# A four-layer graph network on one core: the first group's front begun before the other weights are prepared

## The chip, the cores and the metric

The kernel runs on one core of one Trainium2 chip. The metric is the device time of one execution in microseconds (us). TensorE is called PE here, ScalarE ACT, VectorE DVE, GpSimd POOL and SyncE SP; each has its own stream of instructions, and they meet only in semaphores.

## The reference, cut to what matters

There are 64 graphs of 128 nodes with 256 features, each with a 128x128 adjacency matrix and a node mask. Every graph goes through four layers, each followed by a layer norm over the features of input plus layer:

```
x = norm(x + attention(x, adj, mask, W_qkv, W_out, b_out))   # 8 heads of 64; 0.33*(softmax + adj + exp(-adj)) @ v
x = norm(x + hypergraph(x, adj, W1, b1, gamma, beta, W2, b2))
x = norm(x + diffusion(x, adj, Wv, bv, aw, ab, Wk[0..2], bk))
x = norm(x + relu([x, adj @ x / deg] @ W3.T))
```

All weights are shared by all graphs. They come as plain float32 and the kernel uses them in another form.

## The kernel before, in words

**Tiling.** Two graphs make a group (G = 2), 32 groups in all. The work on a group has a front (the attention layer and the adjacency statistics) and a back (the other three layers). In the steady state one pass of the loop runs the front of group i together with the back of group i-1, interleaved by hand. `group(i, j, n)` on every engine writes such a pass: front of i, back of j, and the first transposes and query/key products of n. The program is: set-up, `group(0, None, 1)` (a front alone), `group(1, 0, 2)`, a hardware loop over 29 more, and two passes at the end.

**Prepared weights.** Each weight matrix is kept as two float32r matrices, a high part (a copy by ACT, `set_hi` counts them) and a low part (weight minus high part, by DVE, `set_lo`; three of them by POOL, `set_pool_lo`). The list `splits` holds them in order: two pieces of W_qkv for queries and keys, two for values, W1, W3, W_out, W2, Wk, and two tiny ones for the gates. Some need more first. W1, W2 and W3 are transposed on PE with the identity (L424, L430, L436). W2 is centred with a row product (L455) that DVE adds (L1082), and the row product with beta (L459) makes `bw_bc`. W3 is centred on DVE (L1058 to L1066). Wk is centred with a column sum on PE (L465, L467), added by DVE (L1072, L1075). The gate vectors come from products on POOL (L1578, L1580), reductions and small sums on DVE (L1088 to L1099) and a column sum on PE (L473).

**The order of set-up.** Engines run their streams in the order in which they are written. PE's `set_up` does the three groups of transposes, waits until the first eight splits are done, transposes x and adj of group 0 (L486, L479), does query/key products 0 and 1 of group 0 (L497, L498, L501), and then the row products and column sums. Behind it each engine calls `set_up_done`, which waits for every split, every copy and every small result. Only then comes `group(0, None, 1)`: query/key products 2 and 3; the masks on ACT (L822, L826) and the gate (L814); scores S of graph 0 and 1 (L523, L531); values v (L408 to L412); the row maximum on DVE (L1197); exp on ACT (L853); normalisation `norm_` on DVE (L1210, eight instructions for a graph); transposes PT (L541) and their copy on ACT (L860); the product with v, PV (L551); its split (L865, L1123); W_out, W_ (L408 to L412); the sum y0 and norm (L1221, L1225, L1133, POOL L1595 to L1602, ACT L871); then AT_ (L516), adjT_ (L479) and ax_ (L571).

**Requests and memory.** SP issues the loads: W_qkv, W2, W1, W3, then adj, row weights, x and mask of group 0, then the gate vectors' inputs, W_out and Wk; ACT and POOL issue some small ones. All raw weights lie in the memory of the work tiles from `work_base` on, which the front of group 0 would write. `early_base` holds the few tiles (adjT, xT0, qk) that may be written during set-up.

Of the kernel before, what the change touches and what calls it, by code (L numbers as in the profile page):

```python
# [14 lines left out]
P = 128  # L15
HEADS = 8
# [10 lines left out]
def gnn_stack_kernel(nc, x, adj, nodemask, W_qkv, W_out, b_out, W1, b1, gamma, beta, W2, b2,  # L27
# [18 lines left out]
    with ctx:  # L46
# [49 lines left out]

        adjTb = at("adjTb", [P, G, P])
        gate = at("gate", [P, G, P])
        aT = pair("aT", [P, G, P])
# [4 lines left out]
        xT2 = pair("xT2", [P, DC, G, P])  # L104
        prob = at("prob", [P, 2, HEADS, P])
        probT = at("probT", [P, G, HEADS, P])
        oT = pair("oT", [P, G, IC, P])
        ys0 = at("ys0", [P, G, D])
        ysb = at("ysb", [P, G, D])
        x1t = at("x1t", [P, G, D])  # L110
        x2 = at("x2", [P, G, D])
        x3 = at("x3", [P, G, D])
        xout = at("xout", [P, G, D])
        resid = at("resid", [P, G, D])
        axT = pair("axT", [P, G, DC, P])
        hid = at("hid", [P, G, DHID])
        hT = pair("hT", [P, G, HC, P])
        hw = at("hw", [P, G, D])
        z01 = at("z01", [P, G, 2, D])
        e1 = at("e1", [P, G, P])  # L120
        e2 = at("e2", [P, G, P])
        al = at("al", [P, G, P])
        alT = pair("alT", [P, G, P])
        yv = at("yv", [P, G, D])
        yT = pair("yT", [P, G, D])
        za = at("za", [P, G, D])
        zb = pair("zb", [P, G, D])
# [16 lines left out]


        NORM0, NORMH, NORM1, NORM2, NORM3 = range(5)
        st = at("st", [P, 5, G, 6])
        mv = at("mv", [P, 5, G, 2])
        rs = at("rs", [P, 5, G, 2])

# [7 lines left out]
        wqkv_raw = at("wqkv_raw", [P, DC, HEADS, 3, DH])  # L158
        wout_raw = at("wout_raw", [P, IC, D])
# [26 lines left out]
        bA, bB, bD, bC, bE, bP, bQ, bR = range(8)  # L186
        bank_wk01, bank_wk2 = 6, 4
# [106 lines left out]
        SET_W2T, SET_W1, SET_W3, SET_CM, SET_BW, SET_WK, SET_MASK, SET_WJ = 1, 2, 3, 4, 5, 6, 7, 8  # L294
        FIRST_FROM_PSUM = len(splits)
        for c in range(DC):
            splits.append((PS[:, 2 + c, :], w1t[0][:, c], w1t[1][:, c], 0.5, (set_pe, SET_W1)))
        for c in range(DC):
            splits.append((PS[:, 4 + c, :].rearrange("p (t o) -> p t o", t=2), w3t[0][:, c], w3t[1][:, c], None,
                           (set_pe, SET_W3)))  # L300
        FIRST_DERIVED = len(splits)
        splits.append((wout_raw[:], wout[0][:], wout[1][:], MIX, (ld_wout, 16)))
        for k in range(HC):
            splits.append((w2c[:, k], w2t[0][:, k], w2t[1][:, k], None, (set_w2c, k + 1)))

        FIRST_ON_POOL = len(splits)
# [3 lines left out]
        POOL_SPLITS = range(FIRST_ON_POOL, len(splits))  # L310
# [36 lines left out]
        def _(sp):  # L347
            sp.dma_start(wqkv_raw[:].rearrange("p c h t d -> p c (h t d)"),
                         W_qkv.rearrange("(c p) n -> p c n", p=P)).then_inc(ld_wqkv, 16)
            sp.dma_start(w2_raw[:], W2.rearrange("(c p) n -> p c n", p=P)).then_inc(ld_w2, 16)  # L350
            sp.dma_start(w1_raw[:], W1.rearrange("(c p) n -> p c n", p=P)).then_inc(ld_w1, 16)
            sp.dma_start(w3_raw[:], W3.rearrange("(c p) n -> p c n", p=P)).then_inc(ld_w3, 16)

            def load_group(i):
                sp.dma_start(adj_in[:], ag[:, bass.ds(i * G, G), :]).then_inc(a_in, 16)
                sp.dma_start(wrow[:], adj[bass.ds(i * G, G), 0:1, :].rearrange("g a m -> (a g) m").partition_broadcast(P))\
                    .then_inc(w_in, 16)
                sp.dma_start(xin[:], xg[:, bass.ds(i * G, G), :]).then_inc(x_in, 16)
                sp.dma_start(mask_bc8[:], mask_rows[bass.ds(i, 1), :].rearrange("a n -> (a n)").partition_broadcast(P))\
                    .then_inc(m_in, 16)  # L360

            load_group(0)
# [4 lines left out]
            sp.dma_start(wout_raw[:], W_out.rearrange("(c p) n -> p c n", p=P)).then_inc(ld_wout, 16)  # L367
            for k in range(3):
                sp.dma_start(wk_raw[:, k], Wk[k].rearrange("(c p) n -> p c n", p=P)).then_inc(ld_wk, 16)
# [35 lines left out]
        def _(pe):  # L405
# [13 lines left out]
            def set_up():  # L419
                pe.wait_ge(ident_ok, 2)  # L420
                pe.wait_ge(ld_w2, 16)
                for k in range(HC):
                    for c in range(DC):
                        last = pe.transpose(PS[:, bQ + k // 2, (k % 2) * D + c * P:(k % 2) * D + (c + 1) * P],  # L424
                                            w2_raw[:, c, k * P:(k + 1) * P], ident[:])
                last.then_inc(set_pe, 1)
                pe.wait_ge(ld_w1, 16)
                for c in range(DC):
                    for k in range(HC):
                        last = pe.transpose(PS[:, 2 + c, k * P:(k + 1) * P], w1_raw[:, k, c * P:(c + 1) * P], ident[:])  # L430
                last.then_inc(set_pe, 1)
                pe.wait_ge(set_w3c, 4)
                for c in range(DC):
                    for t in range(2):
                        for o in range(DC):
                            last = pe.transpose(PS[:, 4 + c, t * D + o * P:t * D + (o + 1) * P],  # L436
                                                w3_raw[:, o, t * D + c * P:t * D + (c + 1) * P], ident[:])
                last.then_inc(set_pe, 1)


                pe.wait_ge(set_copy, 1)
                pe.wait_ge(set_hi, FIRST_DERIVED)
                pe.wait_ge(set_lo, FIRST_DERIVED)
                xT0_(0)
# [597 lines left out]
        def _(dve):  # L1042
# [3 lines left out]
            def set_up():  # L1046
# [55 lines left out]
                for n, (src, hi, lo, factor, (ready, value)) in enumerate(splits):  # L1102
                    if n == FIRST_FROM_PSUM:
                        rows()
                        centre_w3()
# [613 lines left out]
```

## Time and profile before

| what | value |
|---|---|
| median of 3 runs | 1316.94 us (1316.85 to 1317.2) |
| the profiled execution's own time | 1311.29 us |
| its span, first to last instruction | 1309.3 us |
| PE busy | 1251.3 us (96%) |
| DVE, ACT, POOL busy | 1070.5, 973.2, 479.4 us |
| mean granted TensorE clock | 0.987 |

The profile is of one execution. A timeline row gives start, length, engine, line, operation, output and inputs with their sizes, how many instructions are merged, and in brackets how long the engine had been idle and what released it. The granted clock is a share of full speed: 1.00 is 2.4 GHz, 0.50 is 1.2 GHz. Ends of matmuls are modelled, so rows of PE overlap a little; the spacing of starts is the better measure.

### The profile page before, as it was taken

The page shows a single profiled execution, that of the slowest core. Times are in us where ns is not written, and L with a number is a line of the kernel's source. Part 1 is how long each engine was busy: PE and PEld are TensorE (multiplying, and loading weights), DVE is VectorE, ACT ScalarE, POOL GpSimd, SP SyncE. Part 2 cuts the span into 40 slices and gives each one's busy share as a digit, 9 for nine tenths or more (in the row PEclk, how much of TensorE's full clock was granted, in tenths as well). Part 3 has the DMA queues.
Part 4 walks back from the last instruction along what each step waited for, and adds up shares of the span by engine and source line. Part 5 has one row for each costly group of instructions (what it writes and reads, how often), then busy time and mean ns, then how long its engine had stood idle before and what let it go on. Part 6 is the DMA issues. An engine that isn't in the chain of part 4 may idle for free.

```text
span 1309.3 us, 32907 instructions
## 1 busy us (share of the span) xinstructions
PE 1251.3 (96%) x9589; PEld 1112.7 (85%) x9589; DVE 1070.5 (82%) x3399; ACT 973.2 (74%) x2806; POOL 479.4 (37%) x1126
## 2 busy tenths in 40 slices
PE   3699999999999999999999999999999999999996
PEld 3588898888888888889898888988888888888874
DVE  3668898888889888888888888988888898888885
ACT  3467777787777778777878777777877777787773
POOL 2233333344433334343334433333444333343432
PEclk8799999999999999999999999999999999999998
DMA  6000000000000000000001100000001000000000
GB/s 202 10 18 27 26 9 17 25 25 25 25 17 17 17 25 25 25 25 8 23 19 25 25 25 25 8 19 23 25 25 25 20 13 17 25 25 25 17 9 9
DMA packets 44293, 32.52 MB, mean 25 GB/s; under 512 B 8176, under 2 KB 43120, under 8 KB 44272
## 3 DMA queue, kind: packets, MB, share of 16 engines
q1 hardware_dynamic: 42688, 31.47, 8.4%
q0 software_dynamic: 176, 0.52, 0.2%
q10 hardware_dynamic: 1408, 0.27, 0.1%
q8 instruction: 10, 0.16, 0.1%
q14 instruction: 11, 0.09, 0.0%
HBM read 23.87 MB, written 8.39 MB: 25 GB/s over the span
## 4 chain that ended last, share of the span: by engine, by line
PE 88%; issue 3%; DVE 2%; ACT 2%; POOL 1%; DVEq 0%; POOLq 0%; ACTq 0%
PE PS L408 15%; PE PS L409 14%; PE PS L412 14%; PE PS L497 5%; PE PS L551 5%; PE PS L498 4%; PE PS L501 4%; PE PS L531 4%; PE PS L541 4%; PE PS L587 3%; PE PS L571 2%; PE PS L601 2%; PE PS L523 2%; DVE ysb L1372 1%; PE PS L614 1%
## 5 line engine op out<-in xcount | busy, mean ns | idle before, releaser
L1592 POOL TENSOR_TENSOR rs<-mv,eps_c 128x1 f32<-128x1 f32 x256 | 61.8, 242 | 580.9 <-DVE mv L1133 580.5
L1596 POOL TENSOR_TENSOR rs<-rs,mhalf 128x1 f32<-128x1 f32 x320 | 176.3, 551 | 25.3
L853 ACT ACTIVATE prob<-PS,neg_max 128x128 f32<-128x128 f32 x512 | 179.6, 415 | 1.8 <-DVE neg_max L1197 1.8
L497 PE MATMUL PS<-xT_hi,wqk_hi 128*128 128x256 f32 x512 | 141.8, 298 | 5.9 <-DVE wk_lo L1118 4.8
L1210 DVE SCALAR_TENSOR_TENSOR prob<-prob,rl,gate 128x128 f32<-128x128 f32 x512 | 145.4, 346 | 1.4
L498 PE MATMUL PS<-xT_hi,wqk_lo 128*128 128x256 f32 x512 | 135.6, 286 | 0.0
L853 ACT ACTIVATION_READ_ACCUMULATOR prob<-PS,neg_max 128x1 f32 x512 | 130.9, 256 | 0.0
L1244 DVE SCALAR_TENSOR_TENSOR hid<-PS,Dn,b_bc 128x512 f32<-128x512 f32 x64 | 48.1, 751 | 84.0 <-PE PS L412 84.0
L497 PEld LDWEIGHTS PS<-xT_hi,wqk_hi 128*128 128x128 f32 x512 | 98.6, 193 | 12.2 <-issue 10.1
L501 PE MATMUL PS<-xT_lo,wqk_hi 128*128 128x256 f32 x512 | 104.2, 285 | 0.0
L498 PEld LDWEIGHTS PS<-xT_hi,wqk_lo 128*128 128x128 f32 x512 | 99.3, 194 | 0.0
L860 ACT ACTIVATE probT<-PS 128x1024 f32<-128x1024 f32 x64 | 65.9, 1030 | 35.1 <-PE PS L541 35.1
L871 ACT ACTIVATE x<-ysb,rs 128x256 f32<-128x256 f32 x128 | 73.6, 602 | 19.8 <-POOL rs L1602 19.8
L1602 POOL TENSOR_SCALAR rs<-mv,rs 128x1 f32<-128x1 f32 x256 | 68.2, 266 | 53.0 <-POOL rs L1596 52.6
L408 PE MATMUL PS<-wk_hi,xT_hi 128*128 128x260 f32 (+1 forms) x256 | 83.6, 348 | 0.7 <-ACT xT_hi L912 0.7
L836 ACT ACTIVATE qk<-PS 128x512 f32<-128x512 f32 x128 | 73.3, 597 | 13.5 <-PE PS L501 13.3
L409 PE MATMUL PS<-wk_lo,xT_hi 128*128 128x260 f32 (+1 forms) x256 | 83.4, 337 | 0.0
L1197 DVE TENSOR_REDUCE neg_max<-PS 128x8 f32<-128x1024 f32 x64 | 77.9, 1218 | 6.5 <-PE PS L531 6.5
L501 PEld LDWEIGHTS PS<-xT_lo,wqk_hi 128*128 128x128 f32 x512 | 80.9, 193 | 0.0
L1133 DVE BATCH_NORM_AGGREGATE mv<-st 128x2 f32<-128x6 f32 x320 | 56.4, 176 | 25.3 <-DVE st L1249 9.9
L1123 DVE TENSOR_TENSOR xT_lo<-PS,xT_hi 128x256 fp32r<-128x256 f32 (+1 forms) x128 | 70.6, 552 | 4.1 <-ACT xT_hi L808 2.3
L871 ACT ACTIVATE xout<-ysb,rs 128x256 f32<-128x256 f32 x64 | 38.5, 602 | 47.2 <-POOL rs L1602 47.2
(225 smaller groups left out, 4231.3 us busy)
## 6 DMA issues: line engine op xcount, KB each, us to landing
xin<-in_x_dram SPq DMA_DIRECT2D x32, 256.0 KB, 2.7
out_dram<-xout SPq DMA_DIRECT2D x32, 256.0 KB, 2.2
adj_in<-in_adj_dram SPq DMA_DIRECT2D x32, 128.0 KB, 2.1
wrow<-in_adj_dram SPq DMA_DIRECT2D x32, 128.0 KB, 4.6
wqkv_raw<-in_L_gnn_W_qkv_dram SPq DMA_DIRECT2D x1, 1536.0 KB, 7.3
w_raw<-in_L_gnn_W_dram SPq DMA_DIRECT2D x3, 512.0 KB, 11.5
mask_bc<-in_nodemask_dram SPq DMA_DIRECT2D x32, 32.0 KB, 2.8
wk_raw<-in_L_gnn_Wk_dram SPq DMA_DIRECT2D x3, 256.0 KB, 8.3
```

Of the source, the lines that this page charges most:

```text
L408: pe.matmul(dst, lhs[0], rhs[0], start=start, stop=False)
L409: pe.matmul(dst, lhs[0], rhs[1], start=False, stop=False)
L412: return pe.matmul(dst, lhs[1], rhs[0], start=False, stop=stop)
L497: pe.matmul(dst, w[0], xT0[0][:, c], start=(c == 0), stop=False)
L498: pe.matmul(dst, w[1], xT0[0][:, c], start=False, stop=False)
L501: last = pe.matmul(dst, wqk[0][:, c, t, h:h + 2], xT0[1][:, c], start=False, stop=(c == DC - 1))
L836: act.activation(qk[:, 2 * k:2 * k + 2].rearrange("p m g n -> p (m g n)"), PS[:, bank_qk[k], :], copy, scale=SCALE if k < 2 else 1.0).then ...
L853: last = act.activation(prob[:, t, h, :], PS[:, bank, k * P:(k + 1) * P], ACT.Exp, bias=neg_max[:, t, h:h + 1], accum_out=row_sum[:, t, h: ...
L871: act.activation(dst, src, ACT.Identity, scale=rs[:, n, g, 1:2], bias=rs[:, n, g, 0:1]).then_inc(done, 1)
L1197: dve.tensor_reduce(neg_max[:, t], scores, AX_X, ALU.max, negate=True).then_inc(dve_max, 1)
L1210: last = dve.scalar_tensor_tensor(prob[:, t, h, :], prob[:, t, h, :], rl[:, t, h:h + 1], gate[:, t], ALU.mult, ALU.add)
L1596: return pool.tensor_tensor(rs[:, n, g, 1:2], rs[:, n, g, 0:1], mhalf[:], ALU.pow)
```

## The change

Memory: `prob`, `probT` and everything else that the front of group 0 writes now come first after `work_base`; only the raw W_qkv lies over `prob` and half of `probT`. All other raw weights and set-up temporaries are placed from a new `later_base` on, over tiles that are first written by a back or by group 1. The set-up uses other PSUM banks. The splits are reordered to W_qkv, W1, W2, W_out, Wk, W3, gates. `set_up` and `group(0, None, 1)` are replaced by one hand-ordered `first()` on each engine; `set_up_done` comes after it. What is computed is the same.

```diff
+        later_base = place[0]
 ...
         place[0] = work_base
         wqkv_raw = at("wqkv_raw", [P, DC, HEADS, 3, DH])
+        place[0] = later_base
         wout_raw = at("wout_raw", [P, IC, D])
 ...
+            sp.dma_start(xin[:], xg[:, 0:G, :]).then_inc(x_in, 16)
             sp.dma_start(w2_raw[:], W2.rearrange("(c p) n -> p c n", p=P)).then_inc(ld_w2, 16)
+            sp.dma_start(adj_in[:], ag[:, 0:G, :]).then_inc(a_in, 16)
             sp.dma_start(w1_raw[:], W1.rearrange("(c p) n -> p c n", p=P)).then_inc(ld_w1, 16)
 ... (then mask, row weights, Wk, W3, W_out, gate inputs)
```

The new order on PE:

```
            def first():

                pe.wait_ge(ident_ok, 2)
                xT0_(0)
                w2_transposes()
                mask_column()
                w1_transposes()
                adjT_(0)
                pe.wait_ge(set_hi, QK_DONE)
                pe.wait_ge(set_lo, QK_DONE)
                qk_(0, 0)
                pe.wait_ge(dve_xT0, 1)
                qk_(0, 1)
                row_products()
                pe.wait_ge(set_copy, COPY_W2T)
                qk_(0, 2)
                pe.wait_ge(act_qk, 2)
                qk_(0, 3)
                ...
                S_(0, 0)
                ...
                S_(0, 1)
                v_(0, 0)
                v_(0, 1)
                column_sums()
                pe.wait_ge(set_wkc, 4)
                PT_(0, 0)
                pe.wait_ge(act_v, 2)
                xT0_(1)
                PV_(0, 0)
                w3_transposes()
                gate_sums()
                qk_(1, 0)
                qk_(1, 1)
                PT_(0, 1)
                ...
                pe.wait_ge(set_wjc, 1)
                W_(0, 0)
                PV_(0, 1)
                W_(0, 1)
                AT_(0)
                adjT_(1)
                pe.wait_ge(dve_y0, 2)
                ax_(0, 0)
                ...
                ax_(0, 1)
```

On the others, in short (`high(a, b)` and `low(a, b)` are splits a to b-1):

```
ACT:  high W_qk; xT0_(0); high W_v; move w2T; move mask; high W1; adjT_(0); qk_(0, 0..3); move bw;
      mask_(0); gate_(0); high W2; exp_(0, 0); exp_(0, 1); high W_out; v_(0, 0..1); high Wk; PT_(0, 0);
      xT0_(1); OT_(0, 0); high W3; carry(0); PT_(0, 1); qk_(1, 0); BHT_(0); OT_(0, 1); qk_(1, 1);
      high gates; x1_(0, 0); AT_(0); x1_(0, 1); ax_(0, 0..1); adjT_(1)
DVE:  maskf; low W_qk; xT0; low W_v; rows; low W1; centre (W2); incidence; Dsum_(0); cnt_; low W2;
      max_(0); centre_w3; max_(1); centre_wk; rl_ and norm_ of graph 0; rl_ and norm_ of graph 1;
      gate_vectors; low W_out; xT0 of group 1; fOT_(0); centre_gates; low W3; Be0_; Be_; y0_(0);
      Dsum_(1); bn0_(0); fOT_(1); Dn0_; mv0_(0); deg_; y0_(1); bn0_(1); low gates; mv0_(1); ...; ax
POOL: constants; fresid_ (L1609); gate_ (L1616, L1617); gate_products; low Wk; rs0_(0); rs0_(1)
```

## Rows read from the trace of the kernel before

**Rows 1.** Busy time by stretch: us, each engine's busy us, PEclk, DMA share, GB/s.

```profile
0.00:46.26 46.26, 18.65 (x83) 14.71 (x84) 20.08 (x41) 14.59 (x26) 11.15 (x38) 0.84 0.45 143
46.26:78.47 32.21, 25.03 (x186) 21.83 (x187) 14.44 (x45) 17.07 (x55) 5.31 (x10) 0.86 0.07 19
78.47:1309.30 1230.83, 1207.66 (x9323) 1076.15 (x9321) 1036.00 (x3315) 941.57 (x2725) 462.90 (x1079) 1.00 0.07 21
```

**Rows 2.** Waits of the first 80 us: who waited for whom, us, times, longest.

```profile
PE PS L497 <- DVE wk_lo L1118: 4.8, 1, 4.8
```

**Rows 3.** SP's queue: two issues, and us to landing of the requests issued then.

```profile
1.24 0.46 SPq L350 DMA_DIRECT2D w_raw<-in_L_gnn_W_dram  x1
w_raw<-in_L_gnn_W_dram SPq DMA_DIRECT2D x1, 512.0 KB, 10.2
...
1.75 0.46 SPq L351 DMA_DIRECT2D w_raw<-in_L_gnn_W_dram  x1
w_raw<-in_L_gnn_W_dram SPq DMA_DIRECT2D x1, 512.0 KB, 11.5
```

**Rows 4.** Timeline of PE from 0 to 79 us: start us, us, what.

```profile
13.33 1.65 PE L430 MATMUL PS<-ident,w_raw 128*128 128x128 f32 x8
...
31.40 1.99 PE L455 MATMUL PS<-w2T_raw,gamma_bc 128*128 128x256 f32 x8 [0.69 <-ACT qk L836]
...
34.96 1.88 PE L465 MATMUL PS<-wk_raw,mean_w 128*128 128x512 f32 x4
...
69.46 0.36 PE L408 MATMUL PS<-wout_hi,oT_hi 128*128 128x256 f32 x1
...
72.87 0.38 PE L408 MATMUL PS<-wout_hi,oT_hi 128*128 128x256 f32 x1 [0.72 <-ACT oT_hi L865]
```

**Rows 5.** The chain that ended last: one query/key matmul at either clock.

```profile
47.88 0.21 PE PS L497
...
66.67 0.12 PE PS L497
```

**Rows 6.** Timeline of ACT: end of the query/key copies, gate, a split, `bw_bc`.

```profile
33.95 1.59 ACT L794 ACTIVATE w2t_hi<-w2c 128x256 fp32r<-128x256 f32 x4 [1.66 <-DVE w2c L1082]
...
43.78 0.36 ACT L782 ACTIVATE bw_bc<-PS 128x256 f32<-128x256 f32 x1
...
51.76 0.60 ACT L836 ACTIVATE qk<-PS 128x512 f32<-128x512 f32 x1 [1.88 <-PE PS L501]
...
53.81 0.41 ACT L814 ACTIVATE gate<-adj_in 128x256 f32<-128x256 f32 x1
```

**Rows 7.** Timeline of DVE: the steps that the new order puts in a row.

```profile
14.97 1.21 DVE L1058 TENSOR_REDUCE w3m<-w_raw 128x4 f32<-128x1024 f32 x1
...
17.59 1.28 DVE L1118 SCALAR_TENSOR_TENSOR w1t_lo<-PS,w1t_hi 128x512 fp32r<-128x512 f32 x2
...
37.74 1.28 DVE L1072 TENSOR_TENSOR wk_raw<-wk_raw,PS 128x512 f32<-128x512 f32 x2 [2.65 <-PE PS L467]
...
39.61 1.21 DVE L1088 TENSOR_REDUCE wji<-prod 128x4 f32<-128x1024 f32 x1
...
43.45 1.22 DVE L1118 SCALAR_TENSOR_TENSOR wout_lo<-wout_raw,wout_hi 128x1024 fp32r<-128x1024 f32 x1
...
54.72 2.35 DVE L1197 TENSOR_REDUCE neg_max<-PS 128x8 f32<-128x1024 f32 x2 [6.46 <-PE PS L531]
...
62.06 2.19 DVE L1210 SCALAR_TENSOR_TENSOR prob<-prob,rl,gate 128x128 f32<-128x128 f32 x8
```

**Rows 8.** Small DVE instructions beside POOL's, timeline from 38 to 48 us.

```profile
39.77 3.72 POOL L1586 TENSOR_TENSOR wk_lo<-wk_raw,wk_hi 128x512 fp32r<-128x512 f32 x3 [12.11 <-DVE wk_raw L1075]
...
41.45 0.83 DVE L1093 TENSOR_TENSOR gate_c<-bsum,ab_bc 128x1 f32<-128x1 f32 x1
...
46.29 1.40 POOL L1609 TENSOR_TENSOR ys<-xin,bout_bc 128x512 f32<-128x512 f32 x1 [2.80 <-DVE wk_lo L1118]
46.46 1.26 DVE L1148 COPY mcol<-mask_c 128x2 f32<-128x2 f32 x1
```

More of the change, by code:

```diff
@@ L95, in gnn_stack_kernel @@
         work_base = place[0]
+        prob = at("prob", [P, 2, HEADS, P])
+        probT = at("probT", [P, G, HEADS, P])
+        NORM0, NORMH, NORM1, NORM2, NORM3 = range(5)
         adjTb = at("adjTb", [P, G, P])
         gate = at("gate", [P, G, P])
[L99 removed]
         HT = at("HT", [P, G, P])
@@ L1113, in set_up, with centre_gates, low @@
+            def centre_gates():
+                dve.wait_ge(set_pe, SET_WJ)
+                for c in range(DC):
+                    last = dve.tensor_tensor(wji[:, :, c], wji[:, :, c], PS[:, bank_wj, D:D + 2], ALU.add)
+                last.then_inc(set_wjc, 1)
+            def low(a, b):
+                for n in range(a, b):
+                    src, hi, lo, factor, (ready, value) = splits[n]
                     dve.wait_ge(set_hi, n + 1)
@@ L1532, in group, with first @@
                     assert bstep.n == DVE_BSTEPS, bstep.n
-            set_up()
+            def first():
+                (fstep, _, incidence, cnt_, deg_, Be0_, Be_, Dsum_, Dn0_, Dn1_, Dn_, max_, rl_, norm_, fOT_, y0_, bn0_,
+                 mv0_) = front(0)
+                mask_rows_f32()
+                low(0, QK_DONE)
+                front(0)[1]()
+                low(QK_DONE, V_DONE)
+                rows()
+                low(V_DONE, W1_DONE)
+                centre()
+                dve.wait_ge(set_copy, COPY_MASK)
+                incidence()
+                Dsum_(0)
+                cnt_()
+                low(W1_DONE, W2_DONE)
+                max_(0)
+                centre_w3()
+                max_(1)
+                centre_wk()
+                rl_(0, 0)
+                rl_(0, 1)
+                norm_(0, 0)
+                norm_(0, 1)
+                rl_(1, 1)
+                rl_(1, 0)
+                norm_(1, 0)
+                norm_(1, 1)
+                gate_vectors()
+                low(W2_DONE, WOUT_DONE)
+                front(1)[1]()
+                fOT_(0)
+                centre_gates()
+                low(WK_DONE, W3_DONE)
+                Be0_()
+                Be_()
+                y0_(0)
+                Dsum_(1)
+                bn0_(0)
+                fOT_(1)
+                Dn0_()
+                mv0_(0)
+                deg_()
+                y0_(1)
+                bn0_(1)
+                low(W3_DONE, N_SPLITS)
+                mv0_(1)
+                Dn1_()
+                Dn_()
+                back(0)[1](0)
+                back(0)[1](1)
+                assert fstep.n == DVE_FSTEPS, fstep.n
+            first()
             set_up_done(dve)
-            group(0, None, 1)
             group(1, 0, 2)
@@ L1682, in group, with first @@
                     assert bstep.n == POOL_BSTEPS, bstep.n
+            def first():
+                fstep, fresid_, gate_, rs0_ = front(0)
+                pool.wait_ge(pool_const, 10)
+                pool.wait_ge(ld_vec, 16 * 3)
+                fresid_()
+                gate_()
+                gate_products()
+                low()
+                rs0_(0)
+                rs0_(1)
+                assert fstep.n == POOL_FSTEPS, fstep.n
             set_up()
+            first()
             set_up_done(pool)
-            group(0, None, 1)
             group(1, 0, 2)
```

319 lines of the change are left out of this document (170 added, 149 removed).

## The prediction

> **What bounds the kernel now.** I read the busy time by stretch first. From 78.47 us, where PE begins the first pass that has both a front and a back, to the end at 1309.3 us the row shows PE busy 1207.66 of 1230.83 us at full clock [rows 1]: that part is bound by PE. The change leaves its instructions as they are, and I carry it over whole. The two rows before it are what is open. In the first 46.26 us PE works 18.65 us, DVE 20.08 and ACT 14.59; in the next 32.21 us (group 0's front alone) PE works 25.03, DVE 14.44 and ACT 17.07, and the mean clock is 0.84 and 0.86. Nothing is full there. The waits say what separates the two stretches: PE idles 4.8 us until DVE has made the last low part, that of the gates [rows 2]. The question is therefore when the second pass begins, 78.47 us before. A gain there is a gain of the program, once and not per group.
>
> **What goes.** The barrier at 46 us, with the wait of 4.8 us, and the one ahead of the first eight splits. No work is removed: each transpose, product, split and sum is still issued once. What the change can win is the overlap of two chains that ran one behind the other. At the limit, the whole overlap is bounded by DVE: 20.08 + 14.44 = 34.5 us of its work from a first start near 9 us gives 44 us, or 35 us less. I don't expect the limit, because every engine keeps a fixed order; the order is what must be walked through.
>
> **The start, led by requests and PE.** SP issues W2 at 1.24 us and W1 at 1.75 us; they land 10.2 and 11.5 us later, at 11.4 and 13.25 us, so 512 KB take 1.8 us [rows 3]. Two requests are moved ahead of W1, x (256 KB) and adj (128 KB): 384 KB, 1.3 us by the same rate, so W1 lands at 14.5 us. The x transposes (near 10 us) and W2's lie before that and cost nothing on this path; if a request were late they would, one for one. W1's eight transposes take 1.65 us [rows 4], a fifth of a us each, and the two of adj 0.4 us, so the first query/key product starts at 16.7 us. It has 12 matmuls, at 0.21 us each on the low clock and 0.12 on the high [rows 5]. I let the clock rise at 17.5 us, because before it rose within W1's transposes or some 3 to 6 us into a busy stretch; either end is worth 1.3 us. So product 0 ends at 18.5 and product 1 at 20.0. The two row products took from 31.40 to 34.96 us, 3.56 us [rows 4]: 23.5. Products 2 and 3, 24 x 0.12 = 2.9: 26.4, with the last drain 26.6.
>
> **The middle, led by ACT and then DVE.** Before, from the start of the copy of product 3 (51.76) to the end of the gate (53.81 + 0.41) it took 2.46 us; the copy of `bw_bc` (0.36) is now between them [rows 6]. From 26.6 that is 29.4 us. The scores are ready by 30 us, as the masks precede the gate. But W2's high parts now stand between gate and exp on ACT (1.59 us, to 31.0 [rows 6]), and its low parts ahead of the row maximum on DVE: the last of them ends at 31.4. Both exps wait behind that. From here DVE is a single row of work:
> - row maximum 0, half of 2.35 us [rows 7]: 32.6;
> - centring of W3, from 14.97 to 17.59, 2.6 us [rows 7], plus 1.0 us for a collision (below): 36.2;
> - row maximum 1: 37.4;
> - centring of Wk, from 37.74 to 39.61, 1.9 us: 39.3. PE's values and column sums end near 36, so they don't hold it;
> - reciprocals 0.2 and normalisation of graph 0, 2.19 us [rows 7]: 41.7;
> - the same for graph 1: 43.9, plus 3.7 us for a collision: 47.7;
> - gate vectors, 3.84 us from 39.61 to 43.45 less the 0.7 us by which one of them waited there: 50.8;
> - low part of W_out 1.22, x of group 1 and the first PV low part, a little over half of that each, gates 0.2: 53.5.
>
> W_ of graph 0 waits for these (`set_wjc` and the low part of PV), so it starts at 53.5 us. PE arrives at about the same time: its PT copy stands behind Wk's high parts on ACT, to 44.7, then PV and W3's transposes at the low clock (1.9 and 1.7 us by twice their high-clock shares), the gate sums behind the first reduction at 48.9, two query/key products and PT, 53.2. From W_ of graph 0 to W_ of graph 1 it was 72.87 - 69.46 = 3.41 us [rows 4], from there to the second pass 78.47 - 72.87 = 5.60. The small gate split adds 0.3 on DVE. Sum: 53.5 + 3.4 + 5.6 + 0.3 = 62.8 us, against 78.47: **15.7 us less**.
>
> **The two collisions.** The small sum `gate_c` has two inputs in SBUF. It took 0.83 us where its neighbours of that size take 0.15, and it began at 41.45 inside POOL's three products of 1.24 us each (39.77 to 43.49), of which the second ends near 42.3, where `gate_c` ends too. A copy of two columns took 1.26 us and ended with POOL's L1609 [rows 8]. So a small or two-input instruction of DVE can wait for a whole one of POOL. In the new order POOL's gate products (from 31 to 34.8) lie beside the W3 centring, whose small scaling would start at 33.8: 1.0 us. POOL's three low parts of Wk (3.72 us) lie beside the normalisation of graph 1, which reads `prob` and `gate`. No row shows those two together; the ends are 0 and 3.72 us, and I take 3.7 by `gate_c`, the nearest row. With 0, PE is the later one at W_ (52.6) and the gain is 16.6, so this term is worth 0.9 us in the end. The Trainium skill, SBUF — State Buffer, section "Who interferes with whom", says that DVE and GpSimd share one pair of ports, that a DVE instruction with two SBUF inputs contends with a GpSimd one that reads SBUF, and that the loser blocks fully. By that rule the collision is full, as in the sum; the `gate_c` row agrees. It speaks against the placing of the POOL work, not against the overlap.
>
> **The requests moved last.** Gate inputs, W_out, W3 and Wk land later or earlier than before, with the same bytes in total, so the last near 27 us. POOL takes gate inputs at 31, DVE W3 at 32.6, PE Wk at 33.5: covered by 4 us or more. POOL's bias add (L1609) moves to 11 to 13 us, off every chain. SP's next loads of x can go out at once and wait for nobody.
>
> **Rivals.**
> - *The clock stays high and the collisions don't occur.* PE is busy from 28 to 36 us and then idle 5 us; before, short gaps between 53 and 62 us kept it high for a while. Without the low stretch PV and W3's transposes cost 1.8 us less; without collisions the DVE row is 4.7 us shorter. Then W_ starts near 50 us: gain 19 us, 1298 us. For it: no collision of POOL with an instruction as long as the normalising ones is in a row. Against it: a gap like this has shown the low clock in both stretches (0.84 and 0.86) [rows 1].
> - *The clock stays low and W1 is late.* Query/key products 0 to 3 at 0.21 cost up to 44 x 0.09 = 4.0 us more, the two of group 1 another 2.2, a W1 1 us later 1: gain 8.5 to 12 us, near 1307 us. For it: the products at 46 to 52 us ran low throughout, five us into a busy stretch [rows 5]. The Trainium skill, TensorE: Matmul & The Clock Gate, section "What's actually happening", says that the throttled clock is the default and activity lifts it; the low rows behind the wait of 4.8 us agree.
> - *The change does not overlap.* If a load or a fixed wait put PE behind all splits again, the front would follow as before: within 2 us of 1316.9. Against it: the waits in PE's new order ask only for the splits that the next step needs.
> - *Slower.* Work tiles get other addresses, and the passes run the same instructions on them. If an address made one instruction on PE's path dearer, it would be paid in each of the 32 passes (38.5 us each, 1230.83 / 32). From 0.5 us a pass (15.7 / 32) it eats the gain; at 0.8 us the kernel takes 1327 us. No row shows an address with a price, so I give it little.
>
> **How the numbers follow.** The profiled execution took 1311.29 us (span 1309.3); less 15.7 it is 1295.6. The median of the runs shown is 5.65 us above it; less the same 15.7 it is 1301.2 us, my forecast. Chances: gain 14 to 17.5 us, 0.45; larger, 0.24; smaller down to 8.5 us, 0.24; no overlap, 0.03; slower, 0.04. The range takes gains from 11 to 20.5 us: 1296.5 to 1306.0, which leaves out 2 in 10. About 0.2% (2.6 us) is what a measurement of this kernel can tell from no change. Faster by more: 0.94; within: 0.02; slower: 0.04.
>
> **What would show it.** Right: PE's first query/key product near 17 us, the gate's end near 29.4, row maximum 0 near 31.4 behind W2's low parts, W_ of graph 0 near 53.5, the second pass near 63, and 1231 us from there on. The collisions: the small scaling of W3 over 1 us, eight normalising instructions of graph 1 over 3 us longer than those of graph 0. Wrong: query/key products 2 and 3 at 0.21 us, W1 landing after 16 us, a PE wait on DVE of over 5 us ahead of W_, or passes longer than 38.5 us.

## The result and the profile after

| | before | after |
|---|---|---|
| median | 1316.89 us (1314.01 to 1317.2, 4 runs) | 1302.16 us (1301.38 to 1303.38, 4 runs) |
| ratio, 95% interval | | 0.9907 (0.9888 to 0.9926) |
| profiled execution, own time | 1311.29 us | 1303.38 us |
| its span | 1309.3 us | 1301.4 us |

The change is faster, by 14.7 us in the medians, where 15.7 us were forecast; the median lies 1 us from the forecast. But the two profiled executions are only 7.9 us apart. The 6.8 us between the two differences are 5.6 us by which before's profiled execution lies under its median and 1.2 us by which after's lies over its own. Which of the two is the change's worth has to be explained. The page of the profile after, its span and its busy times:

```profile
span 1301.4 us, 32910 instructions
PE 1253.8 (96%) x9589; PEld 1116.7 (86%) x9589; DVE 1074.4 (83%) x3399; ACT 972.1 (75%) x2806; POOL 480.3 (37%) x1126
```

The number of matmuls, and that of instructions on DVE, ACT and POOL, is that of before. Busy time by stretch, after (us of the stretch; then PE, PE's weight load, DVE, ACT and POOL, each busy us; PEclk; DMA share; GB/s), split where the second pass begins, and two stretches of 15 us:

```profile
0.00:70.40 70.40, 45.94 (x267) 40.29 (x268) 38.22 (x85) 30.95 (x81) 17.17 (x47) 0.85 0.34 102
70.40:1301.40 1231.00, 1207.82 (x9324) 1076.42 (x9323) 1036.23 (x3315) 941.16 (x2725) 463.09 (x1079) 1.00 0.07 21
30.00:45.00 15.00, 10.38 (x60) 8.10 (x60) 13.27 (x26) 9.41 (x42) 5.80 (x5) 0.86 0.02 4
45.00:60.00 15.00, 12.28 (x62) 11.14 (x62) 12.36 (x25) 5.67 (x11) 3.85 (x3) 0.50 0.01 1
```

Three things are to be seen. The rest of the program is what it was: 1231.00 us, 1230.83 before [rows 1]. DVE is what the front now waits for from 30 to 45 us, 13.27 us busy of 15. And from 45 to 60 us PE runs at 0.50, the 1.2 GHz level. PE's timeline after (start us, us, what), cut to the milestones:

```profile
15.80 1.97 PE L428 MATMUL PS<-ident,w_raw 128*128 128x128 f32 x8 [0.68 <-DMA w_raw<-in_L_gnn_W_dram]
17.85 0.56 PE L495 MATMUL PS<-xT_hi,wqk_hi 128*128 128x256 f32 x1
...
21.92 1.89 PE L449 MATMUL PS<-w2T_raw,gamma_bc 128*128 128x256 f32 x8
...
44.19 2.08 PE L539 MATMUL PS<-ident,prob 128*128 128x128 f32 x8 [4.19 <-DVE prob L1286]
...
48.34 1.98 PE L549 MATMUL PS<-probT,vh 128*64 128x128 f32 x16 [1.22 <-ACT probT L899]
50.24 1.97 PE L436 MATMUL PS<-ident,w_raw 128*128 128x128 f32 x8
...
55.42 0.79 PE L499 MATMUL PS<-xT_lo,wqk_hi 128*128 128x256 f32 x2 [1.50 <-DVE xT_lo L1199]
...
59.85 1.77 PE L539 MATMUL PS<-ident,prob 128*128 128x128 f32 x8
...
61.38 0.36 PE L405 MATMUL PS<-wout_hi,oT_hi 128*128 128x256 f32 x1
...
70.64 0.36 PE L495 MATMUL PS<-xT_hi,wqk_hi 128*128 128x256 f32 x1
```

The last row is the second pass: 70.64 us, against 78.47 before and 62.8 forecast. So the trace holds a gain of 7.8 us, half of the one that was worked out. DVE's timeline after:

```profile
31.51 4.47 DVE L1192 TENSOR_TENSOR w2t_lo<-w2c,w2t_hi 128x256 fp32r<-128x256 f32 x4 [5.20 <-ACT w2t_hi L836]
35.90 1.21 DVE L1273 TENSOR_REDUCE neg_max<-PS 128x8 f32<-128x1024 f32 x1
...
38.27 0.17 DVE L1141 TENSOR_SCALAR w3m<-w3m 128x4 f32<-128x4 f32 x1
...
42.91 2.19 DVE L1286 SCALAR_TENSOR_TENSOR prob<-prob,rl,gate 128x128 f32<-128x128 f32 x8
...
45.35 5.23 DVE L1286 SCALAR_TENSOR_TENSOR prob<-prob,rl,gate 128x128 f32<-128x128 f32 x8
...
54.68 0.69 DVE L1199 TENSOR_TENSOR xT_lo<-PS,xT_hi 128x512 fp32r<-128x512 f32 x1
```

And POOL's, over the same time:

```profile
31.25 0.73 POOL L1747 TENSOR_TENSOR gate<-gate,adj_in 128x256 f32<-128x256 f32 x1 [17.91 <-ACT gate L853]
32.06 0.79 POOL L1748 TENSOR_TENSOR gate<-gate,mbc 128x256 f32<-128x256 f32 x1
32.81 2.89 POOL L1707 TENSOR_TENSOR prod<-wv_raw,aw_bc 128x512 f32<-128x512 f32 x2
35.66 1.48 POOL L1709 TENSOR_TENSOR bprod<-aw_bc,bv_bc 128x512 f32<-128x512 f32 x1
46.32 3.85 POOL L1717 TENSOR_TENSOR wk_lo<-wk_raw,wk_hi 128x512 fp32r<-128x512 f32 x3 [9.19 <-ACT wk_hi L836]
```

DVE's four low parts of W2 take 4.47 us. They start with POOL's first gate operation and end with its second gate product (32.81 + 2.89 = 35.7), just before the row maximum at 35.90. The eight normalising instructions of graph 1 take 5.23 us and end (50.58) soon after POOL's low parts of Wk (50.17); those of graph 0, beside no POOL instruction, take 2.19. Two questions came out of this: what the start is really bound by, and why the medians moved by more than the traces.

### The profile page after: what moved, and what is told of

Read it like the earlier page. It is cut to its first block, busy times and chain, and to the rows that moved or that the text cites. A ratio compares the mean times of both kernels' runs of the same rounds, so it can differ in the third digit from the quotient of the medians.

```text
span 1301.4 us, 32910 instructions
## 1 busy us (share of the span) xinstructions
PE 1253.8 (96%) x9589; PEld 1116.7 (86%) x9589; DVE 1074.4 (83%) x3399; ACT 972.1 (75%) x2806; POOL 480.3 (37%) x1126
## 4 chain that ended last, share of the span: by engine, by line
PE 93%; DVE 4%; DMA 1%; issue 1%; ACT 1%; POOL 0%; SPq 0%; DVEq 0%; POOLq 0%; ACTq 0%
PE PS L405 15%; PE PS L406 15%; PE PS L409 15%; PE PS L495 5%; PE PS L549 5%; PE PS L499 5%; PE PS L496 5%; PE PS L539 4%; PE PS L529 4%; PE PS L585 3%; PE PS L569 2%; PE PS L599 2%; PE PS L521 2%; DVE ysb L1448 1%; PE PS L612 1%; PE PS L605 1%
## 5 line engine op out<-in xcount | busy, mean ns | idle before, releaser
L1286 DVE SCALAR_TENSOR_TENSOR prob<-prob,rl,gate 128x128 f32<-128x128 f32 x512 | 148.4, 352 | 1.5
```

The lines of the kernel that those rows point to most:

```text
L1286: last = dve.scalar_tensor_tensor(prob[:, t, h, :], prob[:, t, h, :], rl[:, t, h:h + 1], gate[:, t], ALU.mult, ALU.add)
```

## The experiments

All medians, intervals and traces in one table. Each ratio is to the runs of before taken beside it, whose medians were 1315.07 to 1315.9 us. "Second pass" is the start of PE's first query/key matmul of the second pass, "rest" the span less that.

| run | median us (range, n) | ratio (95%) | span | second pass | rest |
|---|---|---|---|---|---|
| before_again | 1315.55 (1311.78 to 1317.5, 10) | 1.0003 (0.9989 to 1.0018) | 1313.3 | 82.36 | 1230.9 |
| after_again | 1302.16 (1301.15 to 1303.89, 4) | 0.9895 (0.9878 to 0.9911) | 1301.2 | 70.47 | 1230.7 |
| wk_late | 1298.73 (1297.84 to 1300.98, 4) | 0.9873 (0.9848 to 0.9897) | 1297.5 | 66.83 | 1230.7 |
| pool_early | 1299.52 (1297.75 to 1301.71, 4) | 0.9872 (0.9848 to 0.9897) | 1299.8 | 66.92 | 1232.9 |
| both | 1299.27 (1298.69 to 1300.24, 4) | 0.9874 (0.9851 to 0.9896) | 1298.3 | 65.34 | 1233.0 |
| warm | 1303.69 (1302.64 to 1304.4, 4) | 0.9917 (0.9891 to 0.9942) | 1302.1 | 70.19 | 1231.9 |
| old_requests | 1306.57 (1306.19 to 1308.19, 6) | 0.9942 (0.9926 to 0.9959) | 1304.4 | 72.28 | 1232.1 |
| xt_early | 1296.83 (1294.13 to 1298.52, 4) | 0.9859 (0.9832 to 0.9887) | 1296.6 | 64.57 | 1232.0 |
| xt_early_warm | 1295.14 (1293.69 to 1295.82, 4) | 0.9852 (0.9826 to 0.9878) | 1293.0 | 61.28 | 1231.7 |
| before_warm | 1313.43 (1308.09 to 1316.28, 10) | 0.9983 (0.9967 to 0.9999) | 1312.0 | 80.21 | 1231.8 |
| warm_start | 1292.8 (1292.1 to 1294.45, 4) | 0.9827 (0.981 to 0.9843) | 1290.8 | 59.87 | 1230.9 |

The rest is not a constant. It is 1230.7 to 1230.9 us in the traces whose second pass begins at the high clock. In `pool_early`, `warm`, `old_requests`, `xt_early`, `xt_early_warm` and `before_warm` the granted clock of its first 5 us is 0.66 to 0.78 and the rest is 1231.7 to 1232.9; the rows of `pool_early` there are

```profile
67.45 0.41 PE L495 MATMUL PS<-xT_hi,wqk_hi 128*128 128x256 f32 x1
67.67 0.41 PE L496 MATMUL PS<-xT_hi,wqk_lo 128*128 128x256 f32 x1
```

and `both` has a stretch at 0.83 from 1245 to 1255 us instead. So up to 2 us of what a trace gains in the start can go again behind it. The start varies by itself, too: `pool_early` and `both` are the same program up to the scores, and the scores begin at 29.88 us in one and at 30.96 in the other (30.43 in the kernel after, 30.12 in `wk_late`). From two second passes less than 1 us apart nothing is concluded.

**Why the medians moved by more: the kernel before, profiled once more** (no edit).

> The kernel of before, unchanged. The change's traces differ by 7.8 us up to the second pass (78.47 against 70.64) while the medians differ by 14.7 us. Theory A: the executions of before differ among themselves in the clock of the first 80 us; this profile then shows a second pass starting 3 to 6 us later than 78.5 us, with more stretches at 0.21 us per query/key matmul, and 1231 us after it. Theory B: the extra time lies in the passes behind; the second pass starts at 78.5 us again and the rest takes 1234 us or more. Theory C: the profile simply runs shorter than the timed executions, for both kernels; then the profiled time is 5 us under the timed ones here too, and the change's four executions should have shown the same gap.

The profiled execution took 1315.25 us, 4.0 more than the first, and its second pass begins 3.9 us later (82.36 against 78.47). The difference lies in the start. PE's timeline:

```profile
33.06 3.78 PE L455 MATMUL PS<-w2T_raw,gamma_bc 128*128 128x256 f32 x8 [0.69 <-ACT qk L836]
```

and the stretch around it:

```profile
30.00:40.00 10.00, 9.31 (x32) 7.29 (x31) 1.66 (x4) 3.13 (x6) 0.00 (x0) 1.00 0.00 0
```

The row product with gamma started at 31.40 us and took 1.99 in the first profile [rows 4]; here it starts 1.66 us later and takes 3.78. That is 3.5 of the 3.9 us: the same matmuls at the low clock for longer. The clock column says 1.00 here, but the matmuls say otherwise. Those of query/key product 1 start 0.21 us apart, which is the low-clock spacing [rows 5]:

```profile
30.04 0.41 PE L497 MATMUL PS<-xT_hi,wqk_hi 128*128 128x256 f32 x1
30.25 0.41 PE L498 MATMUL PS<-xT_hi,wqk_lo 128*128 128x256 f32 x1
```

In these traces the column reads 1.00 from the start up to its first value below 1.00, whatever the spacing is: in the kernel after, too, it is 1.00 from 15 to 20 us over matmuls 0.21 us apart. So the 0.84 of [rows 1] is too high, and a 1.00 before the first lower value is no evidence below; the lengths of PE's rows are.

Of the 10 executions of this run and the 13 of before beside it, the times go from 1311.61 to 1317.5 us: 4 below 1312, 6 from 1314.9 to 1315.4, the other 13 from 1315.69 up. The profile on which the forecast rested (1311.29) is of the short kind, and the change's gain is measured from the middle, near 1315.5. The mean granted clock on record for each execution separates them too: 0.987 or 0.988 for the four short ones, 0.983 or 0.984 for six from 1314.95 to 1315.76, and 0.989 or 0.990 for twelve from 1315.25 to 1317.37 (one more, the longest, has 0.982). The execution profiled here has 0.990, so by its clock it is the shortest of the long kind. The kind at 0.983 was not profiled, and what makes it differ is open. Beside `after_again` before's median was 1315.44 us, and the gain 13.3.

**Does POOL's work on Wk cost the normalisation of graph 1?** The low parts of Wk are held until DVE has normalised both graphs (calls are put on one line here and below):

```diff
                 fresid_(); gate_(); gate_products()
+                pool.wait_ge(dve_attn, 4)
                 low()
```

> The kernel after the change, with POOL's low parts of Wk held back until the normalisation of graph 1 is done. Port theory: the eight normalising instructions of graph 1 fall from 5.2 to 2.2 us. If DVE's row is what PE waits for at W_, the second pass comes 3 us sooner (67.6 against 70.6); if PE at the low clock is what binds there, only the 1.5 us by which PE waited for DVE's low part of x come back (69.1). Rival, the 5.2 us have another cause (semaphores, PSUM): the eight still take 5 us.

DVE's timeline:

```profile
31.20 4.48 DVE L1192 TENSOR_TENSOR w2t_lo<-w2c,w2t_hi 128x256 fp32r<-128x256 f32 x4 [5.20 <-ACT w2t_hi L836]
...
45.05 2.19 DVE L1286 SCALAR_TENSOR_TENSOR prob<-prob,rl,gate 128x128 f32<-128x128 f32 x8
```

The normalisation of graph 1 is back at 2.19 us, so all of its 3.04 us extra were POOL's low parts; W2's low parts, beside other POOL work, stay at 4.48. The second pass begins 3.8 us earlier and the median falls by 3.4, where the forecast valued the collision at 0.9 us. The collision did not go whole, and it is not the whole of the gain. POOL's low parts now lie beside the gate vectors, and there

```profile
49.00 0.84 DVE L1174 TENSOR_TENSOR gate_c<-bsum,ab_bc 128x1 f32<-128x1 f32 x1
```

takes 0.84 us, where it took 0.16 in the kernel after. The low part of x of group 1, for which PE waits, comes 2.6 us sooner (52.08 against 54.68). From there to W_ of graph 0 PE takes 4.8 us instead of 6.0, as some of the matmuls between run at the high clock. Together that is the 3.8.

**And do POOL's gate and gate products cost W2's low parts?** The products go first, and the gate waits for W2's low parts:

```diff
-                fresid_(); gate_(); gate_products()
+                fresid_(); gate_products()
+                pool.wait_ge(set_lo, W2_DONE)
+                gate_()
                 low()
```

> The kernel after the change, with POOL's gate products ahead of its gate (they run near 26 to 30 us) and the gate held back until DVE has made W2's low parts. Port theory: W2's four low parts take 1.4 to 1.7 us instead of 4.5, row maximum 0 starts at 33 instead of 35.9, and the second pass comes 3 us sooner (67.6). Rival, the low parts wait for ACT's high parts, not for POOL: they still take over 3 us and nothing moves.

```profile
30.96 1.44 DVE L1192 TENSOR_TENSOR w2t_lo<-w2c,w2t_hi 128x256 fp32r<-128x256 f32 x4 [3.32 <-ACT w2t_hi L836]
...
42.45 5.30 DVE L1286 SCALAR_TENSOR_TENSOR prob<-prob,rl,gate 128x128 f32<-128x128 f32 x8
```

Four instructions of W2 take 1.44 us without company and 4.47 with it; the row maximum starts at 32.31 instead of 35.90, of which 0.55 us are an earlier start of this execution. The second pass is 3.7 us earlier. The median falls by 2.6 only. The rest is 2.1 us longer in this trace, 1.5 of it in the stretch with the low-clock products shown above; whether the timed executions lose the same is not shown.

**Both together.**

```diff
-                fresid_(); gate_(); gate_products()
+                fresid_(); gate_products()
+                pool.wait_ge(set_lo, W2_DONE)
+                gate_()
+                pool.wait_ge(dve_attn, 4)
                 low()
```

> Both edits together. If the first 60 us are one chain led by DVE: 6 us sooner than the kernel after (second pass near 64.6). If PE at the low clock binds at W_: 4.5 us (near 66.1), 1297.5 us against 1302.

The two large collisions are gone (1.43, 2.19 and 2.19 us; `gate_c` takes 0.85), and the second pass is at 65.34, only 1.5 us before either alone. DVE's timeline has one reason:

```profile
40.52 1.29 DVE L1153 TENSOR_TENSOR wk_raw<-wk_raw,PS 128x512 f32<-128x512 f32 x2 [2.15 <-PE PS L465]
```

DVE, earlier now, waits 2.15 us for PE's column sums of Wk, which the forecast had 1.4 us ahead of it. PE came late to them: this execution reached the scores 0.5 us later than the kernel after, and then ran most of them at the low clock (1.43 and 1.95 us for 16 matmuls, against 1.07 each in `pool_early`). The low part of x of group 1 starts at 52.12, no sooner than in `wk_late` (52.08) or `pool_early` (51.85). What `both` gains over them is PE's clock behind it: 3.3 us from there to W_, against 4.8 and 5.1. So on DVE's row the two collisions don't add up, because without them DVE waits for PE. The median, 1299.27, does not tell the three runs apart.

**Is the low clock from 45 to 60 us what sets PE?** After the column sums PE does 34 transposes whose result nobody reads:

```diff
                 column_sums()
+                pe.wait_ge(act_exp, 2)
+                for n in range(34):
+                    pe.transpose(PS[:, 3, 0:128], ident[:], ident[:])
                 pe.wait_ge(set_wkc, 4)
```

> The kernel after the change with 34 transposes of the identity into a free bank put into PE's idle stretch behind the column sums (they compute nothing that is used). Clock theory: the clock then stays high past 44 us; PT, x of group 1, PV and W3's transposes take half, the query/key products of group 1 0.12 us a matmul once DVE's low part of x is there (55.4 us), and the second pass begins 2.5 to 3 us sooner (near 68 against 70.6). Rival, PE only waits for DVE there: W_ of graph 0 stays at 61.4 and nothing moves; or the padding costs, if the clock falls in spite of it (8 us instead of 4): 3 us later.

```profile
40.64 3.93 PE L788 MATMUL PS<-ident 128*128 128x128 f32 x34
...
48.87 1.98 PE L549 MATMUL PS<-probT,vh 128*64 128x128 f32 x16 [1.90 <-ACT probT L902]
```

A miss. The filling runs at 0.12 us each and keeps the gap closed, but PV still runs low (1.98 us for 16) after the next wait, 1.90 us for ACT's copy. The mean clock of 45 to 60 us rose from 0.50 to 0.77 and the second pass moved by 0.5 us; the median is 1.5 us higher, with ranges that overlap. The row that decides is a later one:

```profile
55.95 0.80 PE L499 MATMUL PS<-xT_lo,wqk_hi 128*128 128x256 f32 x2 [2.46 <-DVE xT_lo L1202]
```

PE now waits 2.46 us for the low part of x of group 1, where it waited 1.50. What it does sooner ahead of this wait is lost in it. So the low clock ahead of the wait did not set PE's arrival at W_; the wait did, and the clock of the 20 query/key matmuls and PT behind it.

**What is the new order of requests worth?** SP's order of before on the kernel after (requests named by what they load):

```diff
-W_qkv, x, W2, adj, W1, mask, row weights, Wk, W3, W_out, gate inputs
+W_qkv, W2, W1, W3, adj, row weights, x, mask, gate inputs, W_out, Wk
```

> The kernel after the change with SP's requests in the order of before (x is the sixth, near 17 us, instead of the second, at 11.5). The new order on PE begins with the transposes of x, so everything behind waits. If the request order carries its part: PE begins near 17, W1's transposes near 19.5 instead of 15.8, and the second pass begins 3.5 to 5.5 us later (near 75). Rival, the start is hidden behind later waits: within 1 us of 70.6.

PE's timeline:

```profile
17.59 1.09 PE L484 MATMUL PS<-ident,xin 128*128 128x128 f32 x4 [17.59 <-DMA xin<-in_x_dram]
...
20.61 1.16 PE L428 MATMUL PS<-ident,w_raw 128*128 128x128 f32 x8
```

With x requested behind 3 MB of weights PE has nothing to do until 17.59 us, where it begins at 11.5 in the kernel after. Yet the scores begin only 2.8 us later, because W1 has landed and the clock is already at its high level when PE gets to it (eight transposes in 1.16 us, against 1.97, and both products behind them at 0.12 us a matmul). The second pass is only 1.6 us later, as PE's clock was higher behind the wait for x of group 1 (4.8 us to W_, against 6.0). The median is 4.4 us higher. The two profiled executions are 2.9 us apart: 1.6 in the start and 1.4 in the rest, whose first 5 us ran at 0.69; and the kernel after's was 1.2 us above its median.

**Is it xT_lo that PE waits for?** `both`, and x of group 1 is split before the gate vectors:

```diff
                 norm_(1, 1)
+                front(1)[1]()
                 gate_vectors(); low(W2_DONE, WOUT_DONE)
-                front(1)[1]()
```

> As the run with both POOL edits, and DVE makes the low part of group 1's x right behind the normalisation, ahead of the gate vectors. PE waited for it until 52.8 us in that run, with the query/key products and PT behind it. If that wait is what binds: the second pass begins 2.5 us sooner than with both (62.8 against 65.3). If DVE's row up to the gates' sums binds W_ instead: under 1 us.

```profile
40.00:55.00 15.00, 12.86 (x70) 11.91 (x71) 12.49 (x35) 7.40 (x16) 3.73 (x3) 0.54 0.01 2
```

The wait went, but the second pass is only 0.8 us earlier than in `both`, and this execution began its scores 0.75 us earlier. PE's clock was 0.54 from 40 to 55 us, and the products of group 1 simply ran at the low spacing from an earlier start. The median is 2.4 us under that of `both`. The same with filling in both places, 34 transposes after the column sums and 14 after query/key product 3:

```diff
                 qk_(0, 3)
+                for n in range(14):
+                    pe.transpose(PS[:, 4, 0:128], ident[:], ident[:])
 ...
                 column_sums()
+                pe.wait_ge(act_exp, 2)
+                for n in range(34):
+                    pe.transpose(PS[:, 3, 0:128], ident[:], ident[:])
```

> The same with two paddings on PE, 34 transposes behind the column sums and 14 behind query/key product 3, so that no idle stretch is left that lets the clock fall before 47 us. Second pass near 61 to 62; the four executions should differ by less than those of the others, as the clock is what differs among them. Rival: the padding delays the scores by up to 0.5 us and wins nothing.

```profile
15.00:30.00 15.00, 13.79 (x91) 13.10 (x92) 4.55 (x14) 6.25 (x14) 3.78 (x3) 1.00 0.57 194
30.00:45.00 15.00, 13.31 (x108) 11.11 (x108) 12.76 (x36) 12.44 (x46) 1.81 (x3) 1.00 0.01 3
45.00:60.00 15.00, 12.00 (x110) 10.63 (x105) 11.22 (x29) 6.78 (x16) 5.44 (x9) 1.00 0.06 16
```

```profile
44.71 1.09 PE L549 MATMUL PS<-probT,vh 128*64 128x128 f32 x16 [1.41 <-ACT probT L904]
...
51.69 0.35 PE L405 MATMUL PS<-wout_hi,oT_hi 128*128 128x256 f32 x1 [0.28 <-DVE wji L1188]
```

Now PE runs high here: PV takes 1.09 us instead of 1.98, and the products of group 1 go at 0.12 us a matmul. W_ of graph 0 starts at 51.69, which is DVE's time (PE waits 0.28 us for it). Against `xt_early` the second pass is 3.3 us earlier and the median 1.7 us lower. `warm` alone gave nothing, and there PE waited for x of group 1. But this run has 14 transposes more than `warm` besides the other orders on DVE and POOL, so what the order and what the second filling did is not separated.

**Does filling alone help the kernel before?** The same kind of transposes, in the set-up of the kernel before (the edit in words):

```diff
+60 of them ahead of W2's transposes
 ...
+27 ahead of PE's wait for set_wji
 ...
+38 after the gates' column sum
```

> The kernel of before with transposes of the identity (not used by anything) in PE's three idle stretches of set-up: 60 from the start, 27 ahead of the gates' column sum, 38 ahead of the barrier. If the clock of the first 80 us is what spreads the executions of before over 1311.6 to 1317.5 us: the second pass begins at 71 to 74 us (against 78.5 and 82.3), the time is 1305 to 1308 us, and the executions lie within 2 us of each other. Then a good part of what the change wins can be had without it. Rival, the spread is in the passes: the time is lower by under 2 us and the spread stays.

```profile
12.56 1.09 PE L426 MATMUL PS<-ident,w_raw 128*128 128x128 f32 x8 [1.36 <-DMA w_raw<-in_L_gnn_W_dram]
14.36 1.97 PE L432 MATMUL PS<-ident,w_raw 128*128 128x128 f32 x8 [0.70 <-DMA w_raw<-in_L_gnn_W_dram]
...
33.91 3.78 PE L457 MATMUL PS<-w2T_raw,gamma_bc 128*128 128x256 f32 x8 [0.69 <-ACT qk L842]
...
50.90 0.36 PE L503 MATMUL PS<-xT_hi,wqk_hi 128*128 128x256 f32 x1 [0.58 <-issue]
```

```profile
20.00:40.00 20.00, 14.48 (x51) 11.52 (x50) 3.64 (x7) 5.79 (x11) 3.73 (x3) 0.54 0.22 73
```

Behind the first filling W2's transposes ran high (1.09 us for eight) and W1's, after 0.70 us of waiting, low (1.97). The clock was at 0.54 from 20 to 40 us all the same, the row product ran low (3.78 us), and the times still spread over 8 us (1308.09 to 1316.28). The last filling did its work: from the barrier's end (50.90) to the scores (55.67) it took 4.8 us, 7.1 in the first profile of before and 6.6 in the second. The median fell by 2.0 us. So this filling does not give the change's gain; and since the clock wasn't held in the first 40 us, the run can't say what before would take if it were.

**The kernel after, once more**, and the best version: `xt_early_warm` with 60 transposes more, from the moment at which the identity is there:

```diff
                 pe.wait_ge(ident_ok, 2)
+                for n in range(60):
+                    pe.transpose(PS[:, 4, 0:128], ident[:], ident[:])
```

> The kernel after the change once more, for its median and its spread beside the others on this chip: 1301 to 1303.5 us. If W_ of graph 0 waits for PE at the low clock here too, the second pass begins near 70.6 us; if this execution has a higher clock from 45 to 61 us, up to 3 us sooner.

> The best version so far (both POOL edits, x of group 1 early, two paddings) with 60 transposes of the identity from PE's start to the arrival of x. W1's transposes take 0.9 us less, and those of x and the first ten query/key matmuls run high too: the gate ends 2 us sooner, the second pass begins near 58.7 instead of 61, 1293 us. Rival: W1's landing and the row products hold the row as before, and it is under 0.5 us.

The kernel after repeats: 1302.16 us again. Its trace answers more than that. From 50 to 55 us its clock was 0.93, where it was 0.50 in the first profile, and still the second pass begins at 70.47 us, within 0.2 us:

```profile
55.41 0.80 PE L499 MATMUL PS<-xT_lo,wqk_hi 128*128 128x256 f32 x2 [2.46 <-DVE xT_lo L1199]
```

PE waits 2.46 us for x of group 1 instead of 1.50, and from 55.41 on both traces are alike. For `warm_start`:

```profile
16.29 1.09 PE L428 MATMUL PS<-ident,w_raw 128*128 128x128 f32 x8 [1.58 <-DMA w_raw<-in_L_gnn_W_dram]
```

W1's transposes take 1.09 us instead of 1.97 and the second pass begins at 59.87, 1.4 us before that of `xt_early_warm`. This version takes 1292.8 us: 9.4 us less than the kernel after and some 22.6 us less than before (1315.44 beside it).

## Why the prediction was right or wrong

**The result was right, the working half right.** That the median came within 1 us of the forecast of 1301.2 us was luck: two errors of opposite sign. The start was worked out 7.8 us too short (second pass at 62.8, measured 70.64). And the medians show 6.8 us more gain than the profiles, because before's profiled execution was 4 to 5.6 us shorter than its usual ones, and after's 1.2 us longer than its median; after's own spread is 2.7 us (1301.15 to 1303.89 over eight executions). The forecast subtracted the same 15.7 us from both; that "less the same 15.7" holds only if the start that the profile shows is the usual one. It wasn't, as `before_again` shows.

By steps:

- **The rest carried over whole: right.** 1231.0 against 1230.83 us [rows 1]. No address became dearer.
- **First query/key product at 16.7 us: 17.85.** W1 was requested at 3.02 us, 1.27 later than before, and landed 12.7 us later, where it had taken 11.5 [rows 3]; its transposes start at 15.80, and 14.5 had been worked out. The sum counted 1.3 us for x and adj ahead of it; 2.5 would have been needed. Why the landing itself took 1.2 us longer was not tested. From 15.80 to the product it took 2.05 us, by the sum 2.2.
- **The clock rises at 17.5: 20.3 us.** Product 0 ran at 0.21 us throughout, product 1 at 0.12. That is 0.85 us more than the sum had; product 3 ends at 28.44 instead of 26.6, and the gate, as worked out from there, 1.8 us later. The size of the clock's part lies within what was named (1.3 us to either end).
- **W2's low parts end at 31.4, row maximum 0 from there: 35.90.** 1.8 us of this are the later gate. The other 2.7 are the first step whose mechanism failed. The step put nothing on W2's low parts and had POOL's gate products beside the W3 centring. But POOL's two gate operations and its first two gate products, from 31.25 to 35.7 us, lay right beside the W2 low parts, which have two inputs in SBUF: 3.0 us, as `pool_early` shows (1.44 us without company). The scaling of W3, where 1.0 us was put, took 0.17 us at 38.27: POOL's last product had ended at 37.1. The collision was right, its place wrong, and its price 3.0 instead of 1.0.
- **PE's column sums end near 36: 40.0.** Most of the scores ran low from 30.64 us on (1.94 and 1.68 us for 16 matmuls). In the kernel after this cost nothing, since DVE came to them at 40.78; in `both` DVE waited for them.
- **Graph 1's normalisation 3.7 us longer: 3.04.** Right in place and nearly in size; `wk_late` shows it gone. POOL's side gave little: its three low parts took 3.85 us against 3.72 [rows 8]. The Trainium skill, SBUF — State Buffer, section "Who interferes with whom", says that an instruction of DVE with two SBUF inputs contends with one of GpSimd that reads SBUF, and that the lock on the shared ports is exclusive; both places agree with that, 1.44 to 4.47 and 2.19 to 5.23 us.
- **DVE's row ends at 53.5: 56.1 us.** After the errors above had offset each other in part (2.7 from W2's low parts and 1.8 from the start, less 1.0 at W3, 0.7 at the normalisation and 0.2 over the rest), this was 2.6 us late.
- **"PE arrives at about the same time, 53.2": 61.4.** This is the step that cost most: 5.3 us beyond DVE's lateness. PE waited for PT's copy (1.22), then for x of group 1's low part until 55.42, since DVE makes it behind the gate vectors and W_out; query/key products 0 and 1 of group 1 ran at 0.21 us each throughout (clock 0.50 from 45 to 60), and PT after them. The working had PE take these products from 48.9 us on and did not ask when DVE would give it `xT_lo`, nor price all 24 at the low clock. Its own row for DVE had the answer: `xT_lo` ends there at 50.8 + 1.2 + 0.7 = 52.7 us, and 20 matmuls and PT behind it take PE 3.3 us at the high clock (`both`) and 6.0 at the low one, so W_ could not start before 56.0 to 58.7. Of the rivals it is the second's term ("the two of group 1 another 2.2") that came true, together with a wait that no case had. That the wait is what binds, and not the clock ahead of it, `warm` and `after_again` show: both were faster ahead of it and waited 2.46 us.
- **From W_ to the second pass 9.3 us: 70.64 - 61.38 = 9.26.** The 3.4, 5.6 and 0.3 us hold.

The rival "clock low and W1 late" described the trace best, but not fully: it gave a gain of 8.5 to 12 us, and the trace shows 7.8. W1 was 1.3 us late and group 1's products were low, as it said; of products 0 to 3 only one was low (about 1 of its 4.0 us); and neither the 3 us on W2's low parts nor the wait for `xT_lo` was in it. The medians show 14.7 because of the spread of before. So the likeliest case holds for the median, and the rival comes nearer to the mechanism. What remains open is what sets the three kinds of before's executions apart, and at what clock the unprofiled one starts.

## What to carry to other kernels

When a hand-made order overlaps two chains, list for every engine not only how long its row is but which results the other engines read from the middle of it: here PE's row looked as long as DVE's, and waited for a split of 0.7 us that DVE made behind the work on two other weights. Keep work of POOL that reads SBUF away from runs of DVE instructions with two SBUF inputs: each overlap of this kind cost 3 us here, and a semaphore wait on POOL got 2.4 to 3 us of it back (0.7 came again at `gate_c`). Beside DVE's reductions the same POOL work cost nothing (the row maximum 1.21 us, the reduction into `wji` 1.21); beside a small copy with one input it did [rows 8]. And before a profile's start-up is used as the base of a sum, see whether other executions of the same kernel start as it does; the spread of the runs (6 us before, 3 after) says so at once.

## What the runs showed that was not expected

- The kernel's start-up alone spreads before's executions over 6 us (1311.61 to 1317.5), and the steady part of the two profiled ones is the same to 0.1 us. Between these two the difference is when PE's clock rises; for the others only the mean clock is on record.
- A granted clock of 1.00 in the stretches before the first recorded change is no evidence: in the second profile of before the matmuls at 30 to 33 us are spaced 0.21 us, the low clock, under a column that says 1.00.
- The granted clock at the hand-over to the steady part goes with up to 2 us of time: the rest of the program is 1230.7 to 1230.9 us behind a high start of the second pass and 1231.7 to 1232.9 behind a low one.
- One filled gap did not keep the clock: `warm` had PV at the low level again behind the next wait, of 1.90 us. With three fillings (`warm_start`) all of PE's rows from W2's transposes to the second pass run high, and each of W1's transposes took 0.14 instead of 0.25 us. The Trainium skill, TensorE: Matmul & The Clock Gate, section "What's actually happening", says that activity lifts a clock that is low by default; `warm_start` agrees (W2's transposes behind the first filling 1.09 us instead of 1.97). In `before_warm`, with 125 transposes more, the clock was nevertheless at 0.54 from 20 to 40 us.
- Removing two collisions of 3 us each gave 3.8 and 3.7 us of start-up singly, but 5.3 together, and no more in the median than either alone.
